# Causal attention on one Trainium2 core: value products for eight heads at a time, and the output projection two slots sooner

## What is computed

```
h = layernorm(x + multihead(x, x, x, sa_wq, sa_wk, sa_wv, sa_wo, causal=True), ln1_g, ln1_b)
h = layernorm(h + multihead(h, encoding, encoding, ca_wq, ca_wk, ca_wv, ca_wo, causal=False), ln2_g, ln2_b)
ff = relu(h @ ff_w1.T + ff_b1) @ ff_w2.T + ff_b2
h = layernorm(h + ff, ln3_g, ln3_b)
# then, with q = h and k = v = ctx:
w = softmax((q @ Wq + bq) @ (k @ Wk + bk).T / 16);  y = w @ (v @ Wv + bv)
out = y * sigmoid(concat(q @ Wq + bq, y) @ Wg + bg) * mask + q
```

## Time and profile before

| | |
|---|---|
| median of 3 runs | 867.31 us (866.52 to 868.8) |
| profiled execution | 866.2 us |
| its span | 864.4 us |
| mean granted TensorE clock | 0.955 of full speed |
| TensorE matmul busy | 780.5 us (90%) |
| TensorE weight loads busy | 649.9 us (75%) |
| VectorE busy | 662.7 us (77%) |
| ScalarE busy | 439.0 us (51%) |
| GpSimd busy | 485.8 us (56%) |
| chain that ended last, TensorE's share | 62% |
| chain that ended last, VectorE's share | 17% |

### The profile page before, as it was taken

How to read it: one execution, slowest core, us unless ns; L and a number is a source line. 1 busy time by engine, 2 the same in 40 slices (tenths; PEclk the granted TensorE clock), 3 DMA queues, 4 the chain that set the end, 5 groups by cost and what they waited for, 6 DMA issues and landing times.

```text
span 864.4 us, 19936 instructions
## 1 busy us (share of the span) xinstructions
PE 780.5 (90%) x7214; PEld 649.9 (75%) x7232; DVE 662.7 (77%) x1517; ACT 439.0 (51%) x921; POOL 485.8 (56%) x598
## 2 busy tenths in 40 slices
PE   5896899999999898878889999999999889999885
PEld 4765678887887676555468888888877779989874
DVE  3535767878878988668889999998888776977774
ACT  4431355656565565556555555555544543445442
POOL 2401457777677666544356666566555666657542
PEclk9999989999999999799699999999999998999978
DMA  8297679768857764345422222222200020012222
GB/s 272 47 371 178 115 124 146 152 119 136 142 100 135 121 102 87 78 99 110 94 54 54 54 53 54 54 54 54 53 2 10 2 70 8 29 55 68 68 82 77
DMA packets 105297, 79.58 MB, mean 92 GB/s; under 512 B 43256, under 2 KB 101962, under 8 KB 104942
## 3 DMA queue, kind: packets, MB, share of 16 engines
q1 hardware_dynamic: 101434, 72.02, 40.6%
q10 hardware_dynamic: 3764, 6.29, 2.0%
HBM read 27.03 MB, written 12.97 MB: 46 GB/s over the span
## 4 chain that ended last, share of the span: by engine, by line
PE 62%; DVE 17%; issue 5%; SPq 2%; ACT 2%; DMA 2%; POOL 1%; POOLq 0%; DVEq 0%; ACTq 0%
PE a_misc L87 13%; PE a_pair L87 11%; PE a_s L1006 8%; PE a_pair L793 4%; PE a_s L769 4%; PE a_pair L967 4%; PE a_pair L811 3%; PE a_s L767 3%; PE a_pair L952 3%; PE a_s L929 2%; PE a_pair L1105 2%; PE a_s L87 2%; DVE c_z L1512 1%; PE a_pair L814 1%; DVE a_nm L1408 1%
## 5 line engine op out<-in xcount | busy, mean ns | idle before, releaser
L1408 DVE TENSOR_REDUCE a_nm<-a_s 128x2 f32<-128x512 f32 (+1 forms) x192 | 127.1, 678 | 53.8 <-PE a_s L769 53.2
L1921 POOL TENSOR_TENSOR c_hidden<-c_hid,c_hidden 128x256 fp32r<-128x256 f32 x128 | 95.9, 749 | 119.7 <-DVE c_hid L1650 119.6
L1171 ACT ACTIVATE a_pT<-a_pair 128x512 f32<-128x512 f32 x192 | 113.9, 597 | 86.4 <-PE a_pair L793 79.0
L1266 ACT ACTIVATE a_pT<-a_pair 77x512 f32<-77x512 f32 x128 | 75.9, 593 | 145.7 <-PE a_pair L952 141.2
L1006 PE MATMUL a_s<-c_w,c_hidden 128*128 128x256 f32 x768 | 119.5, 296 | 0.0
L87 PE MATMUL a_pair<-c_fxh,c_w 128*128 128x256 f32 x512 | 101.7, 292 | 13.8 <-DVE c_hid L1650 13.8
L1828 POOL TENSOR_SCALAR_AFFINE_SELECT a_pT<-a_pT 128x256 f32<-128x256 f32 (+1 forms) x192 | 91.4, 493 | 32.3 <-ACT a_pT L1171 31.9
L1006 PEld LDWEIGHTS a_s<-c_w,c_hidden 128*128 128x128 f32 x768 | 101.0, 194 | 0.4 <-issue 0.4
L87 PEld LDWEIGHTS a_pair<-c_fxh,c_w 128*128 128x128 f32 x512 | 80.1, 193 | 16.8 <-DVE c_hid L1650 16.7
L1650 DVE TENSOR_SCALAR c_hid<-a_pair,ff_b_col 128x256 f32<-128x256 f32 x128 | 61.2, 479 | 28.2 <-ACT c_hidden L1292 28.1
L793 PE MATMUL a_pair<-a_sq,a_sk 98*128 98x256 bf16 (+1 forms) x512 | 77.1, 255 | 6.4 <-ACT a_pT L1171 6.3
(11 more groups left out here) (258 smaller groups left out, 2153.4 us busy)
## 6 DMA issues: line engine op xcount, KB each, us to landing
a_sq<-a_parts SPq DMA_DIRECT2D x96, 128.0 KB, 4.4
a_sk<-a_parts SPq DMA_DIRECT2D x96, 128.0 KB, 4.6
a_sq<-c_parts SPq DMA_DIRECT2D x96, 128.0 KB
x<-in_xT SPq DMA_DIRECT2D x16, 256.0 KB, 6.5
res<-in_x SPq DMA_DIRECT2D x16, 256.0 KB, 5.6
out<-g_fin SPq DMA_DIRECT2D x16, 256.0 KB, 2.1
a_sk<-kc_parts SPq DMA_DIRECT2D x96, 38.5 KB
fold_rows<-x_fold ACTq DMA_DIRECT2D x1, 2496.0 KB, 11.4
```

The source lines that it names most:

```text
L1171: nc.scalar.activation(pT[g % NPT][:], stps[g % 2][:], ACT.Exp).then_inc(s_exp, 1)
L1266: nc.scalar.activation(pT[g % NPX][0:SC], st_ps[0:SC, :], ACT.Exp).then_inc(c_exp, 1)
L1408: nc.vector.tensor_reduce(nm[c % 2][:, QT * heads[0] + qt:QT * heads[-1] + qt + 1:QT], sps[g % 2][:].rearrange("p (h k) -> p h k", h=len(h ...
L1921: nc.gpsimd.tensor_tensor(hl(m), hid[n % NHID][:], f32(hh(m)), ALU.subtract).then_inc(c_hl, 1)
```

## The change

- `values` takes a pair of four-head groups per visit, in slots 4 and 10 alone; the first of the two moves three slots later (`AV_LAG` 25 to 28), the second stays where it was.
- `NPT` goes from 6 to 8 `pT` tiles. The two new ones lie on the bias rows `ln2_b`, `ln3_g` and `ln3_b`, `ff_b2`. So these four rows are no longer loaded at the start but after the last value product (`s_av` at 64), in SP's order behind the cross values of sequence 3, and GpSimd waits for them (`rows_loaded`) in the first `shifted_rows2`.
- `out_slot` goes from slot 10 to 8 for all sequences but the last, so the output projection stands in slots 8 and 9 and the residual in slot 9. All waits of `project_out` stay.

The diff, without the lines that only rename a count or repeat `t.rows`:

```diff
@@ context_products: SP
-            for n, v in t.rows.items():
-                sp.dma_start(v[:], A(n).partition_broadcast(P)).then_inc(small, 16)
+            for n in t.first_rows:
+                sp.dma_start(t.rows[n][:], A(n).partition_broadcast(P)).then_inc(small, 16)
@@ causal_cross_feed_gated
-    NPT, NVP, NPX, NHID = 6, 4, 4, 3
-    ST_LAG, EXP_LAG, SEL_LAG, AV_LAG = 20, 21, 22, 25
+    NPT, NVP, NPX, NHID = 8, 4, 4, 3
+    ST_LAG, EXP_LAG, SEL_LAG, AV_LAG = 20, 21, 22, 28
...
-    pT = [sb(f"pT{i}", [P, 512], F32) for i in range(NPT)]
+    pT = [sb(f"pT{i}", [P, 512], F32) for i in range(NPT - 2)]
+    pT += [nc.alloc_sbuf_tensor_at(f"a_pT{NPT - 2 + i}", [P, 512], F32, offset=t.place[n]) for i, n in enumerate(("ln2_b", "ln3_b"))]
...
     def out_slot(c):
 
-        return (c + 3, 4) if c == B - 1 else (c + 3, 10)
+        return (c + 3, 4) if c == B - 1 else (c + 3, 8)
@@ SP, loads of the cross stage
+                if c == NSTK - 1:
+                    sp.wait_ge(s_av, 4 * B)
+                    for v, src in t.later_rows:
+                        sp.dma_start(v[:], src.partition_broadcast(P)).then_inc(rows_loaded, 16)
                 load_queries(c)
@@ TensorE
-            def values(rr):
-                c, r = divmod(rr, 4)
+            def values(p):
+                c, j = divmod(p, 2)
                 if not real(c):
                     return
-                j, ro = divmod(r, 2)
-                if rr == 0:
+                if p == 0:
                     pe.wait_ge(v_ones, NVP)
-                pe.wait_ge(s_sel, 3 * rr + 3)
-                if r == 0:
+                pe.wait_ge(s_sel, 6 * p + 6)
+                if j == 0:
                     pe.wait_ge(s_vev, c + 1)
-                if ro == 0:
-                    atleast(pe, s_tr, 2 * (c - 1) + j + 1)
-                col = ro * S
-                for i in range(4):
-                    mt(...)
-                last.then_inc(s_av, 1)
+                atleast(pe, s_tr, p - 1)
+                for ro in range(2):
+                    rr, col = 2 * p + ro, ro * S
+                    for i in range(4):
+                        mt(...)
+                    last.then_inc(s_av, 1)
...
-                if (g - AV_LAG) % 3 == 0:
-                    values((g - AV_LAG) // 3)
+                if (g - AV_LAG) % 6 == 0:
+                    values((g - AV_LAG) // 6)
@@ GpSimd, shifted_rows2
+                if c == 0:
+                    pool.wait_ge(rows_loaded, 16 * 4)
@@ program
+        t.first_rows = ("ln1_g", "ln1_b", "ln2_g")
+        t.later_rows = [(t.rows[n], a["L0_xattn_" + n]) for n in ("ln2_b", "ln3_g", "ln3_b", "ff_b2")]
```

More of the change, by code:

```diff
@@ L205, in _ @@
                 sp.wait_ge(v, 16)
-            sp.wait_ge(small, 16 * (len(t.rows) + len(t.cols) + 1 + 2))
+            sp.wait_ge(small, 16 * (len(t.first_rows) + len(t.cols) + 1 + 2))
         @block.tensor
@@ L238, in _ @@
             square(1, "wvT", "wg2").then_inc(s_w2, 1)
-            pe.wait_ge(small, 16 * (len(t.rows) + len(t.cols) + 1 + 2))
+            pe.wait_ge(small, 16 * (len(t.first_rows) + len(t.cols) + 1 + 2))
             bq, bk, bv = t.cols["bq"], t.cols["bk"], t.cols["bv"]
@@ L576, in causal_cross_feed_gated @@
     c_loaded = [sem("feed_weights") for _ in range(4)]
+    rows_loaded = sem("later_rows")
     c_stacked = [sem("c_stacked") for _ in range(NSTK)]
@@ L795, in scores_turned @@
                 last.then_inc(s_st, 1)
-            def values(rr):
-                c, r = divmod(rr, 4)
+            def values(p):
+                c, j = divmod(p, 2)
                 if not real(c):
                     return
-                j, ro = divmod(r, 2)
-                if rr == 0:
+                if p == 0:
                     pe.wait_ge(v_ones, NVP)
-                pe.wait_ge(s_sel, 3 * rr + 3)
-                if r == 0:
+                pe.wait_ge(s_sel, 6 * p + 6)
+                if j == 0:
                     pe.wait_ge(s_vev, c + 1)
-                if ro == 0:
-                    atleast(pe, s_tr, 2 * (c - 1) + j + 1)
-                col = ro * S
-                for i in range(4):
[L811 to L815, removed]
-                last.then_inc(s_av, 1)
+                atleast(pe, s_tr, p - 1)
+                for ro in range(2):
+                    rr, col = 2 * p + ro, ro * S
+                    for i in range(4):
+                        mt(avps[j][32 * i:32 * i + 32, col:col + S], vpad[c % NVP][:, 0, 8 * j + 4 * ro + i, :],
+                           pT[(3 * rr + i // 2) % NPT][:, i % 2 * S:i % 2 * S + S], start=True, stop=False, skip_group_check=True)
+                    for i in range(4):
+                        last = mt(avps[j][32 * i:32 * i + 32, col + P:col + S], vpad[c % NVP][:, 1, 8 * j + 4 * ro + i, :],
+                                  pT[(3 * rr + 2) % NPT][:, i * P:(i + 1) * P], start=False, stop=True, skip_group_check=True)
+                    last.then_inc(s_av, 1)
             def project_qk(c, i):
```

## The result

| | before | after |
|---|---|---|
| median | 868.05 us (4 runs, 866.52 to 870.03) | 886.78 us (4 runs, 881.96 to 890.62) |
| profiled execution, its span | 866.2, 864.4 us | 883.81, 882.0 us |
| mean granted clock | 0.955 | 0.957 |

The ratio is 1.0223, 95% interval 1.0176 to 1.027: slower by 18.7 us between the medians, 17.6 between the two profiled executions. Forecast were 883.5 us and +16.3.

The account below looks back on a forecast made before the run. TensorE was taken to set the pace by a small margin, VectorE next. Terms -7.0 + 13.8 + 10.5 - 1.5 + 0.5 = +16.3 on 867.3 gave 883.5 us; range for 8 in 10, 868 to 896.

Parts of the forecast that it names:

- Step 1: Value visits on TensorE: half of them go, saving 0.22 us per pair, 0.44 per period, 7.0 us in all.
- Step 2: Output projection at slot 8: TensorE waits 1.25 us for VectorE's second remainder, 11 times, 13.8 us.
- Step 3: Slots 11 to 3: TensorE waits 0.75 us for slot-0 maxima and 0.2 for x's low half, 11 times, 10.5 us.
- The sum of a period: Causal stage, one sequence of 12 slots: 16.63 - 0.44 + 1.25 + 0.95 = 18.4 us.
- Step 4: Exponential tiles in slots 4 and 10: with eight, the exponential's wait for half a visit costs nothing.
- step 6: Four bias row loads later on SP's queue: the next keys come 0 to 1.5 us late, taken as +0.5.
- Step 5: 320 to 400 us: residuals two slots sooner shorten TensorE's waits by 0 to 2.5 us, taken as -1.5.
- Rival A: Slots 5 to 8 and 11 to 2: VectorE gets ahead, only the saving stays, -8.0, so 859 us; chance 0.13.
- Rival B: Wait only at slot 8's projection, none in slots 11 to 3: +5.8, 873 us; chance 0.10.
- Rival C: Causal stage: TensorE's clock also falls, to 0.89 over some 200 us, adding 11, so 894 us; chance 0.12.
- The packing rule: Value visits: packing speeds TensorE but not the emptying of PSUM, so none of the 7.0 us would be kept.

Follow-up runs that it names:

- e7: The change with output projections up to the twelfth sequence in slots 0 and 1 of the next round, value projection in slots 8 and 9: 869.29 us.
- e8: The kernel before, single visits kept, with the same two projection moves as e7: ratio to before 1.0024.
- e5: The change with ScalarE's key projection copy and VectorE's second remainder put ahead of slot 7's exponential and maxima: 875.77 us, ratio to before 1.0117.
- e1: The change with the output projection back in slots 10 and 11; doubled visits, eight tiles and late rows stay: ratio to before 1.0098.
- e4: The kernel before with only the eight exponential tiles and the four late bias rows: 870.3 us, ratio to before 1.0031.
- e2: The kernel before with only the output projection moved to slots 8 and 9: 877.3 us, ratio to before 1.0126.
- e11: The change with the next stage's low weight half in sequence 10 moved from slot 6 to 9 on VectorE: 883.65 us, ratio to before 1.0216.
- e12: The change with the second residual statistic moved from slot 4 to 6 on VectorE in sequences 4 to 9: 887.96 us, ratio to before 1.0253.

## Why the prediction was right, and where it was not

**Step 1, visits.** Right: 0.25 in the timeline for one entry and one exit fewer, and 0.42 a period between e7 and e8, where 0.22 and 0.44 were forecast. But it only shortens the whole once the waits are gone.

**Step 2, the projection.** Right in cause (e5) and size: 1.31 at the weight load (1.06 at the product) for 1.25. The step used VectorE's chain of 4.04 us from the end of the visit, and that is what the trace after shows. Missed was sequence 10: 1.9 us at the load (1.69 at the product), since the weights' instruction in slot 6 lengthens the chain. It stands in the code next to the lines that the step read.

**Step 3, slots 11 to 2.** Right: 0.68 at the loads for the slot-0 maxima (0.50 at the product) and 0.30 for x, 0.8 to 1.0 where 0.95 was forecast. A third wait for maxima, 0.18 at the loads of slot 0, wasn't foreseen. The step says that two output projections stood behind the slot-10 visit; in the timeline before there was one (208.37), the other stood ahead of it (205.48). The sum took out one, so the number doesn't suffer. A part of the reason was incomplete. The step charged the wait to both edits; e1 shows waits for maxima of 0.93 per steady period from the doubled visits alone, in two places, one of them at slot 9, of which the step says nothing.

**The sum of a period** was 18.4 and is 18.53. (The total forecast, 867.3 + 16.3, is 883.6; the prediction rounds it to 883.5.)

**Step 4, tiles, and step 6, rows.** e4 bears out nothing for the tiles: same period to 0.01 us. Its interval, 0.9989 to 1.0073, holds both nothing and the 0.5 us taken for the rows, so the latter stays unmeasured. The exponential does wait for the half visit (1.56 us at 225.40 in the trace after). TensorE doesn't wait for the exponential in the steady part, as forecast; GpSimd does, 30.9 us in 120 to 340 us, without setting the pace.

**Step 5, the residual sooner.** This step failed: no run shows the -1.5 us. It took two waits whose last releaser was a residual for waits that shrink when it comes sooner; what they turn into wasn't followed slot by slot. e2, with the residual sooner and the visits as before, loses 1.0 us from 12 to 15 and 3.3 from n = 15 on. The change itself takes 2.6 less from n = 15 on, but that isn't shown to be the residual's: e1, with the residual where it was, takes 2.2 less, and e11, with the same instructions there as the change, takes 47.2 us, as long as before. What differs between them is in part the granted clock (the last column but two). The stretch from n = 15 on, before, change, e11, e2:

```profile
331.90:378.90 47.00, 37.51 (x400) 26.60 (x403) 33.13 (x77) 27.20 (x54) 26.68 (x43) 0.85 0.44 100
```
```profile
352.90:397.40 44.50, 35.56 (x396) 26.38 (x393) 32.41 (x77) 26.99 (x54) 26.79 (x43) 0.88 0.46 107
```
```profile
351.00:398.20 47.20, 37.04 (x397) 27.45 (x393) 32.65 (x77) 26.86 (x54) 26.41 (x43) 0.86 0.44 101
```
```profile
339.20:389.50 50.30, 37.73 (x399) 27.52 (x401) 32.70 (x77) 26.87 (x53) 26.43 (x43) 0.83 0.39 95
```

Length times what is missing to 1.00 gives some 7.0, 5.3, 6.6 and 8.6 us lost to the clock. So 1.7 of the change's 2.6 us, and 1.6 of e2's 3.3, go with it. Why the clock and the rest differ stays open. From 12 to 15 every variant with either edit loses: the change 2.3 and e2 1.0 at a clock of 1.00, e1 2.4, of which some 1.7 went with a clock of 0.97.

**The account of the profiled executions,** +17.6: n = 3 to 13 +21.5 (forecast 11 x 1.76 = 19.4; n = 10 alone is 2.0 over its share, n = 12 is 1.2 under, the other nine 0.14 each); n up to 2 and n = 14 -1.3, from 15 on -2.6 (forecast for the rest of the visits and the residual -3.7); start of the stage +0.9, everything behind the causal stage -0.9. That the sum came so close is partly luck: the 1.7 us that the clock took in sequence 10 weren't in it, and behind n = 15 the clock took 1.7 us less than before, which wasn't in it either.

**Rival A** needed the chain of seven under 2.93 us; it stayed at 4.04. **Rival B** (the change with waits only at the projection, period near 17.4) did not come: the change has the waits of step 3 as well. e2's 17.23 lies near it by chance, from a wait of 0.41 and one of 0.18 without the visits' saving. **Rival C** put the clock at 0.89 over 200 us, a figure taken from a row of before. The trace shows 1.00 in every steady period, with waits of 1.06 (change) and 1.50 us (e12) in each, and one fall in sequence 10 that lost 1.7 us. By the Trainium skill (TensorE: Matmul & The Clock Gate, "A second HAM failure mode"), which tells of frequent short idles that make the clock swing, this was the case to expect; the trace agrees for one stretch of 3.4 us and not for the stage. **The packing rule** of the Trainium skill (TensorEngine Tiling, "PSUM Bottleneck"), that the emptying of PSUM may become the limit, would have kept none of the saving. In the change's own order TensorE does wait for VectorE to read PSUM, though VectorE is busy only 29.47 of 40 us: what binds is when it reads, not how much. In e7's order nothing of the kind binds, and 0.42 of 0.44 are kept.

## What to carry to other kernels

Two edits that are each read against the schedule before can uncover the same wait: here the removed visit was the cover of the place to which the projection moved, and a third of the growth of a period, 0.63 of 1.90 us, comes only from both together. Before a step is moved forward, count from the last common event how long the other engine needs to what frees its buffer, and look through the code for the periods in which that chain has an extra instruction. And a saving on the pacing engine is kept only in an order in which it waits for nobody; find that order first, then measure the saving against it.

## What the runs showed of the hardware

- The granted TensorE clock fell to 0.50 for 3.4 us behind a wait of 1.69 us in two kernels, 1.4 us behind its end in the change and 0.3 in e12. Single waits of 1.06 and of 1.50 us once per period of 18.5 to 19 us never brought it down. The length of a wait doesn't decide alone: the clock stayed at 1.00 behind 2.15 us in the kernel before, and two waits of 0.6 and 1.3 us, with 1.8 us between their ends, were followed by a fall in e12 and by none in the change.
- A visit's entry and exit, from 128-column products to 32-column ones and back, cost about 0.2 us together: 0.25 in the timeline, 0.42 a period for two visits fewer.
- Work moved into a chain on VectorE overlaps its neighbours: 0.60 us of statistics made the chain 0.44 longer (e12).
